# Attention: when the next batch's first stacks are loaded, after quad 2's maxima instead of after quad 0's key scores

## The chip, the cores and the metric

The kernel runs on one core of a Trainium2 chip. The metric is the time of one execution on the device in microseconds (us). The engines are TensorE (PE, with PEld for its weight loads), VectorE (DVE), ScalarE (ACT), GpSimd (POOL) and SyncE (SP), which here only issues DMAs.

## What is computed

A pre-normalized transformer block: attention with 16 heads over 16 batches of 512 rows of 256, then a feed-forward part with blockwise FP4 quantization.

```python
x_h = x.reshape(b, t, h, d).transpose(0, 2, 1, 3)
xw = jnp.einsum('bhtd,hde->bhte', x_h, w_att_val)
att = jnp.einsum('bhte,bhse->bhts', xw, x_h) / sqrt(d)
att = softmax(att, axis=-1)
vx = x @ wv_w.T + wv_b
o = jnp.einsum('bhts,bhsd->bhtd', att, vx)      # then o @ out_w.T + out_b
...
x = x + attention(layernorm(x))
x = x + ffn(layernorm(x))      # gate, up, silu, down; each operand quantized in blocks of 16
```

The change touches the attention part alone.

## The kernel before

A batch is one of the 16 inputs of 512 rows. Its 16 heads are worked in four **quads** of four heads (g = 0 to 3), and each quad in four **steps** (j = 0 to 3), one for each tile of 128 keys. The engines run unrolled programs of their own, side by side, and meet only at semaphores.

For each quad the scores are computed twice. First the *max scores* (L919, into one of four PSUM banks named `ring`): DVE takes the negated maximum of each row (L1189, `neg_max`). POOL splits these maxima into a high and a low part (L693), DVE turns them (L1198), and ACT stores them to memory (`store_maxima`, L1148, tensor `max_rows`) and loads them back in another shape (`load_maxima`, L1158, tile `max_stack`). Then the *key scores* (L927) with the maxima added by a second matmul (L930): ACT takes the exponential (L1071, `probs`) and PE weighs the values (L952).

The max scores run ahead: during quad g, from its step 1 on, PE computes those of quad g + 2 (`aimed`). So the max scores of quad 0 of the next batch begin at step 1 of quad 2 of this batch, ahead of that step's key scores. ACT stores the maxima of quad g + 1 at step 1 of quad g, and loads them at step 2 of quad g (after its copy of a bank at L1082); at step 2 of quad 1 it also issues the load of a later batch's x (`load_x`, L1162), for batches up to 12.

Both kinds of scores read two tiles of a quad, `x_stack[g]` and `q_stack[g]`: splits of x and of q, laid out by heads. They are made by POOL as `splits` (L727, L729), stored to memory by SP (`store_half`, L199), and loaded in the other layout by SP (`load_stacks`: two DMAs of 256 KB at L162 and four of 128 KB at L172, 1 MB in all). There is one buffer for each g, so the next batch's stacks can be loaded only when this batch's key scores of that quad are done, and PE waits for all six DMAs (`stack_loaded`, L911).

SP's queue in a batch is: for g = 0, the stores of x and q of the first half, the wait for the key scores of quad 0 (`s_ready`), the wait for those stores to land (in `load_stacks`, L177), quad 0's loads; for g = 1, the wait for quad 1's key scores, quad 1's loads, and the store of kept weights (L834); for g = 2, the stores of the second half and quad 2's loads; for g = 3, quad 3's loads and a load of weights (L829). All of SP's DMAs go through one hardware queue, ACT's through another.

Of the kernel before, what the change touches and what calls it, by code (L numbers as in the profile page):

```python
# [14 lines left out]
TT = T // P  # L15
# [3 lines left out]
QUAD = 4  # L19
QUADS = H // QUAD  # L20
PAIRS = 2
ROWS = 2
# [153 lines left out]
def load_stacks(sp, b, g, x_stack, q_stack, x_rows, q_rows, stored, stack_loaded):  # L176
    sp.wait_ge(stored[g * QUAD // HH], STORES * (b + 1))  # L177
    load_x_stack(sp, b, g, x_stack, x_rows, stack_loaded)
    load_q_stack(sp, b, g, q_stack, q_rows, stack_loaded)
# [255 lines left out]
def attention_block(nc, ctx, x, max_rows, w_gate, w_up, w_down, slabs, slabs_kept, first_x,  # L435
# [9 lines left out]
    def sem(name):  # L445
        return ctx.enter_context(nc.semaphore(name))
# [24 lines left out]
    max_loaded = [sem(f"max_loaded{g}") for g in range(QUADS)]  # L471
# [11 lines left out]
    s_ready, p_ready, pv_done, pv_begun, pv_ended, pv_summed = (  # L483
        sem(n) for n in ("s_ready", "p_ready", "pv_done", "pv_begun", "pv_ended", "pv_summed"))
# [54 lines left out]
    def stands(kind, b):  # L539


        if kind == LAST_ROWS:
            return isinstance(b, int) and b == B - 1
        if not isinstance(b, int):
            return True
        if b < 0 or b > B:
            return False
        return {0: kind not in FINISH and kind != "weights", B - 1: kind not in PREPARE and kind != "weights",
                B: False}.get(b, True)
# [67 lines left out]
    def quantizing(b):  # L617

        return not isinstance(b, int) or b < UNITS
# [36 lines left out]
    with nc.Block() as block:  # L656
# [146 lines left out]
        def _(sp):  # L803
# [5 lines left out]
            def store_half(c, a):  # L809
                store(c, a, x_rows, f"x{a}", (xh, xl, xl, xh))  # L810
                store(c, a, q_rows, f"q{a}", (qh, ql))

            def batch(b):
                last = isinstance(b, int) and b == B - 1
                for g in range(QUADS):
                    i = QUADS * b + g
                    if not last:
                        if g % 2 == 0:
                            store_half(b + 1, g // 2)
                        sp.wait_ge(s_ready, QUAD * TT * (i + 1))  # L820
                        load_stacks(sp, b + 1, g, x_stack, q_stack, x_rows, q_rows, stored, stack_loaded)
                        if g == 3 and quantizing(b + 1):
                            sp.wait_ge(w_quantized, b + 1)
                            load_weights(b + 1)
                        if g == 1 and stands("weights", b):
                            store_weights(b)

            def load_weights(b):
                sp.dma_start(w_raw[:, :].rearrange("p (s c) -> p s c", c=P),  # L829
                             slabs[bass.ds(UNIT * b, UNIT)].rearrange("s p c -> p s c")).then_inc(w_loaded, 16)  # L830

            def store_weights(b):
                sp.wait_ge(kept_used, use("weights", b, BY_ACT) + 1)
                sp.dma_start(slabs_kept[bass.ds(UNIT * (b - 1), UNIT)].rearrange("s p c -> p s c"),  # L834
                             w_turned[:, :].rearrange("p (s c) -> p s c", c=P)).then_inc(w_stored, 16)
# [38 lines left out]
            sp.wait_ge(w_copied, 16 * COPIES)  # L874
            load_weights(0)
            batch(0)
            with sp.Fori(1, B - 3) as b:
                batch(b)
            batch(B - 3)
            batch(B - 2)  # L880

# [925 lines left out]
```

## Time and profile before

| | |
|---|---|
| time, median of 3 runs | 1467.87 us (1466.48 to 1468.46) |
| profiled execution | 1475.75 us, its span 1473.8 us |
| busy, share of the span | PE 1425.4 us (97%), DVE 1264.4 (86%), ACT 865.5 (59%), POOL 659.0 (45%) |
| mean granted TensorE clock | 0.989 |
| DMA queues | SP's (q1) 137.22 MB, ACT's (q10) 10.37 MB; mean 100 GB/s |
| attention part | up to about 930 us; a batch takes some 56 us |

Times of rows are microseconds from the start of the span of the profiled execution. A wait is charged to what came last before the waiting instruction could start. The batches are counted from 0.

### The profile page before, as it was taken

Reading aid. Unit: us, or ns where it says so; the run is one execution under the profiler, and the core shown is the slowest. Engines: PE = TensorE matmul, PEld = TensorE weight load, DVE = VectorE, ACT = ScalarE, POOL = GpSimd, SP = SyncE. Lnnn points to the kernel's source line nnn. Section 1 sums busy time; section 2 is a strip of 40 time slices with the busy share of each in tenths; the row PEclk is TensorE's granted clock in tenths of the full one; section 3 lists DMA queues with packets and bytes.
Section 4 is the critical chain, followed back from the end, with each engine's and each line's share of the span. In section 5 each row is a group of like instructions: output and inputs, shape, how many; then the busy total and the mean of one; then the engine's idle time right before and its main releaser. Section 6 shows DMA issues by size and latency. Waiting matters only on the chain. (4 is left out here: it accounts for less than half of the span.)

```text
span 1473.8 us, 32381 instructions
## 1 busy us (share of the span) xinstructions
PE 1425.4 (97%) x8612; PEld 891.5 (60%) x8612; DVE 1264.4 (86%) x2652; ACT 865.5 (59%) x1731; POOL 659.0 (45%) x911
## 2 busy tenths in 40 slices
PE   6789999999999999999999999899999999999999
PEld 4445555555555555555555554577777777777776
DVE  6878888888888888888888887599999999999996
ACT  1667777777777767777777777533333333333332
POOL 2445545545545546546545523243434343433332
PEclk8999999999999999999999999999999999999999
DMA  7846456455455455465465353000000000000000
GB/s 204 234 132 190 123 144 180 122 154 180 122 154 168 132 155 161 123 166 162 125 165 145 117 145 84 0 15 15 18 14 18 14 18 14 18 14 18 14 18 22
DMA packets 99785, 148.09 MB, mean 100 GB/s; under 512 B 21024, under 2 KB 58272, under 8 KB 99744
## 3 DMA queue, kind: packets, MB, share of 16 engines
q1 hardware_dynamic: 82672, 137.22, 32.9%
q10 hardware_dynamic: 17072, 10.37, 3.0%
q8 instruction: 21, 0.34, 0.1%
q14 instruction: 20, 0.16, 0.0%
HBM read 85.02 MB, written 65.27 MB: 102 GB/s over the span
## 5 line engine op out<-in xcount | busy, mean ns | idle before, releaser
L1189 DVE TENSOR_REDUCE neg_max<-ring 128x1 f32<-128x512 f32 x1016 | 636.3, 680 | 96.2 <-PE ring L919 95.8
L1071 ACT ACTIVATE probs<-scores 128x512 f32<-128x512 f32 x1024 | 533.9, 604 | 184.3 <-PE scores L930 158.4
L1704 PE MATMUL gu_bank<-splits,f_x_T 128*128 128x352 f32 x1024 | 313.7, 459 | 0.1
L919 PE MATMUL ring<-x_stack,q_stack 64*128 64x512 f32 x1016 | 230.1, 449 | 24.5 <-DVE neg_max L1189 11.4
L952 PE MATMUL ring<-probs,v_quad 128*32 128x512 f32 x2048 | 247.9, 602 | 0.2
L1704 PEld LDWEIGHTS gu_bank<-splits,f_x_T 128*128 128x128 f32 x1024 | 189.6, 190 | 95.3 <-ACT f_x_T L1678 0.5
L927 PE MATMUL scores<-q_stack,x_stack 64*128 64x512 f32 x1024 | 207.9, 399 | 10.6 <-DMA max_stack<-max_rows 8.2
L919 PEld LDWEIGHTS ring<-x_stack,q_stack 64*128 64x128 f32 x1016 | 97.8, 186 | 177.2 <-DVE neg_max L1189 114.2
L930 PE MATMUL scores<-max_stack,max_ones 64*128 64x512 f32 x1024 | 203.9, 391 | 0.0
L1394 POOL TENSOR_TENSOR f_small<-f_small,eps 128x1 f32<-128x1 f32 x64 | 43.0, 671 | 296.0 <-DVE f_small L1361 296.0
L1663 ACT ACTIVATE h_T<-h_bank 128x256 f32<-128x256 f32 (+1 forms) x128 | 56.0, 487 | 169.9 <-PE h_bank L1718 169.9
L1726 PE MATMUL y_bank<-splits,h_T 128*128 128x256 f32 x640 | 148.9, 380 | 0.6 <-ACT h_T L1663 0.6
L952 PEld LDWEIGHTS ring<-probs,v_quad 128*32 128x32 f32 x2048 | 54.0, 109 | 124.5 <-issue 78.3
L1726 PEld LDWEIGHTS y_bank<-splits,h_T 128*128 128x128 f32 x640 | 116.7, 190 | 14.4 <-DVE x_all L1579 0.8
L927 PEld LDWEIGHTS scores<-q_stack,x_stack 64*128 64x128 f32 x1024 | 98.3, 186 | 32.7 <-ACT probs L1071 17.6
L693 POOL TENSOR_TENSOR max_cols<-neg_max,one 128x16 fp32r<-128x16 f32 x64 | 13.8, 216 | 227.0 <-DVE neg_max L1189 227.0
L930 PEld LDWEIGHTS scores<-max_stack,max_ones 64*128 64x128 f32 x1024 | 98.4, 186 | 18.9
L1445 POOL TENSOR_TENSOR hq<-h_level,h_scale 128x704 f32<-128x704 f32 x63 | 87.3, 1386 | 24.4 <-DVE h_level L1438 24.4
L716 POOL TENSOR_TENSOR pv_rows<-pv_more,pv_rows 128x512 f32<-128x512 f32 x63 | 80.8, 1282 | 36.0 <-ACT pv_more L1077 35.8
L1678 ACT ACTIVATE f_x_T<-x_bank 128x256 f32<-128x256 f32 x64 | 24.5, 383 | 117.8 <-PE x_bank L1692 117.8
L708 POOL TENSOR_TENSOR x_all<-x_all,out_bias 128x256 f32 (+1 forms) x64 | 47.1, 735 | 103.0 <-DVE x_all L1257 102.7
L1432 DVE SCALAR_TENSOR_TENSOR h_level<-h_mag,h_units 128x704 f32<-128x704 f32 x63 | 56.2, 891 | 39.7 <-ACT h_mag L1427 39.7
(144 smaller groups left out, 2014.1 us busy)
## 6 DMA issues: line engine op xcount, KB each, us to landing
x_rows<-splits SPq DMA_DIRECT2D x128, 256.0 KB, 3.9
x_stack<-x_rows SPq DMA_DIRECT2D x126, 256.0 KB, 4.0
q_stack<-q_rows SPq DMA_DIRECT2D x248, 128.0 KB, 4.0
q_rows<-splits SPq DMA_DIRECT2D x64, 256.0 KB, 2.2
out_dram<-x_all SPq DMA_DIRECT2D x64, 128.0 KB, 1.7
x_all<-in_L_attn_x_dram ACTq DMA_DIRECT2D x14, 512.0 KB, 6.9
w_raw<-slabs SPq DMA_DIRECT2D x14, 192.0 KB, 4.0
slabs_kept<-w_turned SPq DMA_DIRECT2D x14, 192.0 KB, 6.1
```

Source lines behind the costliest of these rows:

```text
L716: pool.tensor_tensor(pv_rows[g % 2][:, :], pv_more[:, :], pv_rows[g % 2][:, :], ALU.add)\
L919: pe.matmul(max_bank(b, g, ROWS * n + m)[:, :], row_tile(q_stack[q], m)[:, p, s * P:(s + 1) * P], row_tile(x_stack[q], m)[:, p, :], start= ...
L927: pe.matmul(scores[ROWS * p + m][:, :], row_tile(x_stack[g], m)[:, p, j * P:(j + 1) * P], row_tile(q_stack[g], m)[:, p, :], start=True, st ...
L930: pe.matmul(scores[ROWS * p + m][:, :], row_tile(max_ones, m)[:, 0, :], row_tile(max_stack[g % 2], m)[:, p, :], start=False, stop=True).th ...
L952: m = pe.matmul(bank(tile)[VW * h:VW * h + VW, :], v[q][:, j, h, :], probs[j][:, k, :], start=(j == steps[0]), stop=(j == steps[1]))
L1071: act.activation(probs[j][:, k, :], scores[k][:, :], ACT.Exp).then_inc(p_ready, 1)
L1189: dve.tensor_reduce(neg_max[q % 2][:, at:at + 1], max_bank(b, g, k)[:, :], AX.X, ALU.max, negate=True).then_inc(m_used, 1)
L1432: dve.scalar_tensor_tensor(out=level, in0=mag, scalar=SHIFT_MIN, in1=units, op0=ALU.max, op1=ALU.subtract)\
L1445: pool.tensor_tensor(blocks(out), blocks(level), spread(scale, BLK), ALU.mult).then_inc(done, 1)
L1663: act.activation(h_T[1 - u][:, first:end, :], h_bank[k][:, 0:end - first, :], ACT.Copy).then_inc(h_moved, 1)
L1704: m = pe.matmul(gu_bank[c][:, :], x_T[u][:, a, :], gate_up_T[:, a, c * CH:(c + 1) * CH], start=(a == 0), stop=(a == HALVES - 1))
L1726: m = pe.matmul(y_bank[:, :], h_T[u][:, k, :], down_T[k][:, :], start=(k == 0), stop=(k == len(SLICES) - 1))
```

## The change

SP's wait ahead of the loads of quad 0's stacks for batch b + 1 is another one: instead of "quad 0's key scores of batch b are done" it is "the maxima of quad 2 of batch b are back in `max_stack`" (`max_loaded[2]`). The other quads keep their wait. Nothing else is changed.

```diff
                     if not last:
                         if g % 2 == 0:
                             store_half(b + 1, g // 2)
-                        sp.wait_ge(s_ready, QUAD * TT * (i + 1))
+                        if g == 0:
+
+                            sp.wait_ge(max_loaded[2], 16 * ROWS * (b + 1))
+                        else:
+                            sp.wait_ge(s_ready, QUAD * TT * (i + 1))
                         load_stacks(sp, b + 1, g, x_stack, q_stack, x_rows, q_rows, stored, stack_loaded)
```

## Rows read from the trace of the kernel before

**Rows 1.** Waits of the whole run: us in total, times, longest us

```profile
PE ring L919 <- DMA q_stack<-q_rows: 9.1, 3, 4.3
PE scores L927 <- DMA max_stack<-max_rows: 8.2, 7, 1.8
PEld scores L927 <- DMA max_stack<-max_rows: 2.6, 2, 1.9
```

**Rows 2.** Timeline of PE, batch 5: start us, us, engine, line, op, times

```profile
345.44 1.92 PE L952 MATMUL ring<-probs,v_quad 128*32 128x512 f32 x16
...
351.16 0.40 PE L927 MATMUL scores<-q_stack,x_stack 64*128 64x512 f32 x2
...
354.30 0.50 PE L919 MATMUL ring<-x_stack,q_stack 64*128 64x512 f32 x2
```

**Rows 3.** Timeline of ACT, batch 5

```profile
344.02 0.55 ACTq L1148 DMA_DIRECT2D max_rows<-max_turned  x1
...
347.64 0.77 ACTq L1158 DMA_DIRECT2D max_stack<-max_rows  x2
348.69 0.42 ACTq L1162 DMA_DIRECT2D x_all<-in_L_attn_x_dram  x1
```

**Rows 4.** Timeline of ACT, batch 7

```profile
454.54 0.56 ACTq L1148 DMA_DIRECT2D max_rows<-max_turned  x1
...
459.49 0.65 ACTq L1158 DMA_DIRECT2D max_stack<-max_rows  x2
```

**Rows 5.** Timeline of PE, batch 7

```profile
455.96 1.92 PE L952 MATMUL ring<-probs,v_quad 128*32 128x512 f32 x16
...
463.20 0.50 PE L927 MATMUL scores<-q_stack,x_stack 64*128 64x512 f32 x2 [1.37 <-DMA max_stack<-max_rows]
...
466.41 0.50 PE L919 MATMUL ring<-x_stack,q_stack 64*128 64x512 f32 x2
```

**Rows 6.** Timeline of SP, batch 7: quad 0's x loads, then quad 1's

```profile
453.00 1.17 SPq L162 DMA_DIRECT2D x_stack<-x_rows  x2
...
459.44 1.14 SPq L162 DMA_DIRECT2D x_stack<-x_rows  x2
```

**Rows 7.** Tile q_stack, batch 7, quad 0: issues, landing

```profile
L172 SPq DMA_DIRECT2D q_stack<-q_rows x4: 370/415/535, 454.3 to 456.0; - x4
...
DMA to landing us min/median/max: 4.0/4.1/4.1
```

**Rows 8.** Tile q_stack, batch 7, quad 1

```profile
L172 SPq DMA_DIRECT2D q_stack<-q_rows x4: 316/370/443, 460.8 to 462.3; - x4
...
DMA to landing us min/median/max: 6.0/6.1/6.3
```

**Rows 9.** Tile q_stack, batch 13, quad 1

```profile
L172 SPq DMA_DIRECT2D q_stack<-q_rows x4: 421/458/583, 796.7 to 798.2; - x4
...
DMA to landing us min/median/max: 4.3/4.3/4.5
```

**Rows 10.** Timeline of SP, batch 0: quad 0's x loads, then quad 1's

```profile
65.03 1.15 SPq L162 DMA_DIRECT2D x_stack<-x_rows  x2
...
68.37 1.38 SPq L162 DMA_DIRECT2D x_stack<-x_rows  x2
```

**Rows 11.** Tile q_stack, batch 0, quad 0

```profile
L172 SPq DMA_DIRECT2D q_stack<-q_rows x4: 408/456/582, 66.2 to 67.8; - x4
...
DMA to landing us min/median/max: 6.1/6.3/8.2
```

**Rows 12.** DMA issues of the page: KB each, median us to landing

```profile
out_dram<-x_all SPq DMA_DIRECT2D x64, 128.0 KB, 1.7
```

**Rows 13.** Timeline of PE, batch 0

```profile
76.02 0.80 PE L919 MATMUL ring<-x_stack,q_stack 64*128 64x512 f32 x2 [4.02 <-DMA q_stack<-q_rows]
```

**Rows 14.** Timeline of PE, batch 13

```profile
800.99 3.61 PE L952 MATMUL ring<-probs,v_quad 128*32 128x512 f32 x16
```

**Rows 15.** Stretch: us, busy PE, PEld, DVE, ACT, POOL, granted clock, DMA share, GB/s

```profile
76.00:80.00 4.00, 3.98 (x14) 2.44 (x15) 2.31 (x5) 2.06 (x4) 0.23 (x1) 0.50 0.97 324
```

## The prediction

> **What bounds the kernel now.** I read the shares of busy time first: TensorE (PE) is busy 97% of the span, the VectorE (DVE) 86%. A share over the whole span doesn't say what one DMA wait is worth, so the next view is the waits of the whole run. The reader is to see there two DMA waits of PE: it waits for the maxima that come back from memory (8.2 us at the matmuls and 2.6 us at the weight loads, nine waits, 10.8 us in all), and three times for a stack of q (9.1 us) [rows 1].
>
> Then two batches side by side, each from the moment at which ACT issues the store of quad 2's maxima; I call that moment M. In batch 5 nothing waits: M is 344.02, the maxima's load is issued at 347.64 (M+3.6), the load of a later x at 348.69 (M+4.7), quad 2's key scores start at 351.16, and at 354.30 (M+10.3) PE runs the first max scores of quad 0 of the **next** batch, the first reader of the stacks that this change moves [rows 2, 3]. In batch 7 M is 454.54 and the maxima's load goes out only at 459.49, so the store took up to 4.9 us; the key scores start at 463.20 and the next batch's first max scores at 466.41, M+11.9 [rows 4, 5]. From the step at 455.96 that takes 10.45 us; the same steps of batch 5, from 345.44, take 8.86 us [rows 2, 5]. So a stall here of some 1.4 us costs about 1.6 us of the batch: nothing gives it back. That is my exchange rate, one for one, for every wait of PE below.
>
> What delays the store is plain in SP's queue: quad 0's loads for the next batch are issued at 453.00, the rest of quad 0's loads lands at 460.1, and quad 1's follow at 459.44 [rows 6, 7]. The change takes the first group out of the way of the maxima.
>
> **The change part by part.** (1) *Removed:* SP no longer waits for quad 0's last key scores. That wait is covered: the batch's second quad has to be running before quad 2's maxima can come back. Cost nothing.
>
> (2) *The maxima go undisturbed.* The 10.8 us of waits go, nearly all of them in these places. In batch 13 such a wait was followed by a group of value matmuls that took 3.61 us where the same group took 1.92 in batch 5; that 1.7 us goes too [rows 1, 2, 14]. Gain: 12.5 us at most, over 15 batches.
>
> (3) *The loads of quad 0 start later.* M+3.6 for the maxima's load as in batch 5, then its way. The traces bound that: below by the fastest landing on the page, 1.7 us [rows 12]; above by 3.7 us, from 459.49 to 463.20, when quad 1's loads ran beside it [rows 4, 5]. I take 2.2 us, near the fast end, because SP's queue is now empty meanwhile (SP itself stands in the new wait). With 0.1 us for SP to react, the loads go out at M+5.9, where batch 7 had them at M−1.5 [rows 4, 6].
>
> (4) *How long they take.* A quad's stacks are six DMAs, 1 MB, and PE waits for all of them. Four rows give the time from first issue to last landing; the q loads start 1.2 to 1.3 us behind the x loads [rows 6, 7]. Quad 0 in batch 7, alone: 453.00 to 456.0+4.1, 7.1 us [rows 6, 7]. Quad 1 in batch 13, where no x is loaded any more: 795.5 (796.7 less 1.2) to 798.2+4.5, 7.2 us [rows 9]. Quad 1 in batch 7, beside the load of x: 459.44 to 462.3+6.3, 9.2 us [rows 6, 8]. Quad 0 in batch 0, beside the load of x and with quad 1's loads right behind it at 68.37: 65.03 to 67.8+8.2, 11.0 us [rows 10, 11]. The new place has both neighbours: the load of x is issued at M+4.7, 1.2 us ahead of these loads, and quad 1's loads are queued right behind them, since their own condition is long true. So the nearest rows are the last two; I take 9.0 us, because part of x is moved before the stacks' bytes come, and keep 7.1 and 11.0 as ends. In batches 13 and 14 (no x) I take 7.8 us.
>
> The Trainium skill gives another price for the same megabyte ("DMA: Bandwidth & Descriptors", section "Anatomy of one DMA", a fit of 2.0 us plus bytes over 436 GB/s, stated for DMAs from GpSimd): an estimate by that page is 4.4 us, and the stacks would be there at M+10.3, just when PE asks. This case's trace speaks against it by 7.1 us for the least disturbed quad.
>
> (5) *The new wait.* Arrival at M+14.9, PE asks at M+10.3: 4.6 us in each of 12 batches (1 to 12), 55 us. Batches 13 and 14: M+13.7, 3.4 us each, 7 us. In batch 0 PE already waits for these stacks until 76.02, so only the later issue counts [rows 13]: 2 us. Batch 15 loads nothing. Sum 64 us. What is queued behind SP's waiting instruction is quad 1's loads, the store of the kept weights and the store of the second half of x; PE wants quad 1's stacks a whole quad later (some 14 us), and the second half's loads come after another store that is bound by GpSimd, so these have cover. PE is strictly in order here: behind its wait stand the key scores of the running quad, so ACT (exponentials) and DVE (maxima) run dry too.
>
> (6) *TensorE's clock.* During batch 0's wait the granted clock went down, and 76 to 80 us ran at 0.50, that is 1.2 GHz instead of 2.4: 4 us of work at half speed, 2.0 us lost [rows 15]. Batch 13's slow group is the same size (1.7 us). The new waits are as long as batch 0's. I take a fall in 11 of 14 batches at 1.8 us each: 20 us. Ends: none, and 14 times 2.1, 29 us.
>
> The Trainium skill describes this pattern ("TensorE: Matmul & The Clock Gate", section "HAM oscillation — how this bites in real kernels"): matmuls separated by DMA waits restart at the low clock each time. Batch 0's row agrees; batch 7's short wait shows no slow group after it.
>
> **Sum.** +64 −12.5 +20 = +71 us. The profiled run takes 1475.75 us (span 1473.8); that makes 1546.8. The profiled run is 7.9 us above the median of 1467.87, so against the median: 1539 us.
>
> **The rivals.**
> *A. Faster: the maxima's wait goes and nothing takes its place.* It decides at one point: the six loads must land within 4.4 us of M+5.9. Then only (2) is left, 1467.9 − 12.5, **1455 us**. For it: the waits for the maxima are real, and they are in this very place [rows 1, 5]; and the fit of the Trainium skill named above, "DMA: Bandwidth & Descriptors", would give just that. Against it: no row has less than 7.1 us. Chance 5%.
> *B. No effect.* The loads aren't what holds up the maxima, and the stacks are prefetched early enough. Then 1468 us. It would need the 10.3 us to be wrong; the loads would move by 7 us without a reader. Chance 4%.
> *C. A small loss.* The stacks land 7.1 us after issue, as quad 0's do now: a wait of 2.7 us, 14 times, 38 us, less 12.5, with the clock falling seldom (0 to 10 us): +25 to +36, **about 1498 us**. For it: the present row of exactly these loads. Chance 21%.
> *D. My forecast,* +45 to +95 us: chance 60%.
> *E. A heavy loss.* Batch 0's 11.0 us in every batch: 6.6 us, 14 times, 92 us, less 12.5, and the clock at 29: +109, **1577 us**. A second part may add to it: the traffic that is put off (quad 1's stacks, the half of x) meets the store of quad 3's maxima, at 1.2 us a meeting (8.2 us in seven waits) [rows 1]; I take none of it, since PE's own wait moves that store back as well. Chance 10%.
>
> **How the numbers follow.** The time is D's. To hold 8 in 10 the range takes D and most of C, and E's near part: 1498 to 1572 us. A measurement of this kernel can tell about 0.2% (3 us) from no change. Faster by more: A, 5%. Same: B, 4%. Slower: C, D and E, 91%.
>
> **What would show it.** In the profile after, in the waits of PE: the row for the maxima's stack (8.2 us) gone or near it; a row of the ring's max scores waiting for the stacks (x or q), 14 or 15 times, 3 to 6 us each, in place of three times. In SP's queue, quad 0's x loads about 5.9 us after the store of quad 2's maxima instead of 1.5 us before, with quad 1's some 3.5 us behind them. The granted clock of the attention part below its present level, with groups of value matmuls near 3.6 us. The q loads of quad 0 landing in 5.5 to 6.5 us instead of 4.1. The batches from 57 us to about 61. The feed-forward part unchanged.
> The forecast is wrong if the six loads land in under 6 us (A and C), if the wait for the maxima stays (then they were held up by something else), or if PE makes up for a wait of 4 us where it made up for none of 1.4.

## The result and the profile after

The changed kernel takes 1522.59 us (median of 4 runs, 1520.37 to 1524.88) against 1467.53 us (1466.48 to 1468.46) before: a ratio of 1.037, with a 95% interval of 1.035 to 1.039. It is slower by 55 us; the forecast was 71 us, 1539, with a range of 1498 to 1572. The profiled execution took 1524.11 us, its span is 1522.1. One execution of the first experiment below took 8051.6 us and is left out of its figures.

The shares of the page of after (busy us, share of the span, instructions):

```profile
span 1522.1 us, 32381 instructions
PE 1441.1 (95%) x8612; PEld 902.4 (59%) x8612; DVE 1266.0 (83%) x2652; ACT 867.2 (57%) x1731; POOL 659.4 (43%) x911
```

The work is the same to within 0.2% on DVE and ACT; PE is 16 us busier with as many instructions; the batch table below puts that down to the same work at a lower clock. What is new stands in the waits of the whole run (us in total, times, longest us):

```profile
PE ring L923 <- DMA q_stack<-q_rows: 50.8, 17, 4.6
PEld ring L923 <- DMA q_stack<-q_rows: 15.9, 5, 5.0
PE scores L931 <- DMA max_stack<-max_rows: 1.6, 2, 1.4
PEld scores L931 <- DMA max_stack<-max_rows: 0.5, 1, 0.5
```

Beside [rows 1]: the waits for the maxima have gone from 10.8 us to 2.1, and the matmul of the max scores now waits 17 times for the stacks, 50.8 us, where it waited three times, 9.1 us. (Lines are four further down than before.) One batch of after, number 5, in the order of the engines. ACT (start us, us): the store of quad 2's maxima at M = 360.05, their load, and the load of a later x:

```profile
360.05 0.55 ACTq L1152 DMA_DIRECT2D max_rows<-max_turned  x1
...
363.62 0.65 ACTq L1162 DMA_DIRECT2D max_stack<-max_rows  x2
364.54 0.42 ACTq L1166 DMA_DIRECT2D x_all<-in_L_attn_x_dram  x1
```

SP: quad 0's loads, and quad 1's right behind them:

```profile
365.82 1.17 SPq L162 DMA_DIRECT2D x_stack<-x_rows  x2
367.08 1.97 SPq L172 DMA_DIRECT2D q_stack<-q_rows  x4
369.38 1.14 SPq L162 DMA_DIRECT2D x_stack<-x_rows  x2
```

The tile q_stack of these loads, issues and landing:

```profile
L172 SPq DMA_DIRECT2D q_stack<-q_rows x4: 315/371/532, 367.1 to 368.7; - x4
DMA to landing us min/median/max: 4.4/4.5/4.9
```

PE: its wait, and the same step in batch 4, where the clock stayed up:

```profile
315.35 0.49 PE L923 MATMUL ring<-x_stack,q_stack 64*128 64x512 f32 x2 [3.15 <-DMA q_stack<-q_rows]
...
316.94 1.12 PE L971 MATMUL ring<-raw_x,qw_cols 128*128 128x512 f32 x2
317.90 0.60 PE L988 MATMUL ring<-ident,pv_rows 128*128 128x128 f32 x4
318.58 0.50 PE L923 MATMUL ring<-x_stack,q_stack 64*128 64x512 f32 x2
...
373.74 0.49 PE L923 MATMUL ring<-x_stack,q_stack 64*128 64x512 f32 x2 [3.34 <-DMA q_stack<-q_rows]
...
375.53 2.07 PE L971 MATMUL ring<-raw_x,qw_cols 128*128 128x512 f32 x2
377.40 1.06 PE L988 MATMUL ring<-ident,pv_rows 128*128 128x128 f32 x4
378.39 0.50 PE L923 MATMUL ring<-x_stack,q_stack 64*128 64x512 f32 x2
```

These lines show that the maxima are loaded at M+3.6, as in [rows 3]; the stacks are asked for at M+5.8 and are there at 368.7+4.9 = 373.6, M+13.55; PE begins 0.14 us later, at M+13.7, where the undisturbed batch of before began at M+10.3 [rows 2]. Then comes the second price: the same work, from the first pair of these max scores to the first pair of the next step, takes 3.23 us in batch 4 and 4.65 us in batch 5. The stretches of after (us, busy time of PE, PEld, DVE, ACT, POOL, granted clock, DMA share, GB/s) name the reason:

```profile
316.00:320.00 4.00, 3.92 (x28) 2.34 (x24) 3.97 (x10) 2.98 (x6) 2.30 (x3) 1.00 1.05 286
376.00:378.00 2.00, 2.00 (x5) 0.86 (x5) 1.20 (x4) 1.07 (x3) 0.84 (x1) 0.50 1.07 307
```

### The profile page after: what moved, and what is told of

Its sections match the earlier page's. It is cut to its first block and busy times, and to the rows that moved or that the text cites. A ratio compares the mean times of both kernels' runs of the same rounds, so it can differ in the third digit from the quotient of the medians.

```text
span 1522.1 us, 32381 instructions
## 1 busy us (share of the span) xinstructions
PE 1441.1 (95%) x8612; PEld 902.4 (59%) x8612; DVE 1266.0 (83%) x2652; ACT 867.2 (57%) x1731; POOL 659.4 (43%) x911
## 5 line engine op out<-in xcount | busy, mean ns | idle before, releaser
L923 PE MATMUL ring<-x_stack,q_stack 64*128 64x512 f32 x1016 | 234.9, 458 | 65.5 <-DMA q_stack<-q_rows 50.8
L934 PE MATMUL scores<-max_stack,max_ones 64*128 64x512 f32 x1024 | 207.7, 399 | 0.0
L1730 PEld LDWEIGHTS y_bank<-splits,h_T 128*128 128x128 f32 x640 | 116.7, 190 | 14.4 <-DVE x_all L1583 0.8
L1436 DVE SCALAR_TENSOR_TENSOR h_level<-h_mag,h_units 128x704 f32<-128x704 f32 x63 | 56.2, 892 | 39.5 <-ACT h_mag L1431 39.5
```

Of the source, the lines that this page charges most:

```text
L923: pe.matmul(max_bank(b, g, ROWS * n + m)[:, :], row_tile(q_stack[q], m)[:, p, s * P:(s + 1) * P], row_tile(x_stack[q], m)[:, p, :], start= ...
L934: pe.matmul(scores[ROWS * p + m][:, :], row_tile(max_ones, m)[:, 0, :], row_tile(max_stack[g % 2], m)[:, p, :], start=False, stop=True).th ...
L1436: dve.scalar_tensor_tensor(out=level, in0=mag, scalar=SHIFT_MIN, in1=units, op0=ALU.max, op1=ALU.subtract)\
L1730: m = pe.matmul(y_bank[:, :], h_T[u][:, k, :], down_T[k][:, :], start=(k == 0), stop=(k == len(SLICES) - 1))
```

## Where the 44 us of the batches come from

When every batch is read in this way, before and after, the times from one store of quad 2's maxima to the next one add up to 842.1 us before and 886.5 us after for batches 0 to 14, 44.4 us more. Three terms make them up. First, PE's first max scores of the next batch come later than the undisturbed M+10.3: in after by 39.5 us over batches 1 to 12 (2.8 to 3.5 each), 4.3 us in batches 13 and 14, 2.8 us in batch 0, in all 46.6 us. Second, before had such delays too: 9.8 us in batches 1 to 12, 4.1 in batch 0, 3.6 in batch 13 (its low clock within it), in all 17.5 us, and 2.0 us of low clock behind batch 0's wait. Third, the low clock of after: 11 of 15 batches have a stretch at 1.2 GHz about the end of the wait or behind it. From the next batch's first max scores to the next M, a batch with the clock up takes the same time before and after (44.7 us in batches 1 to 11); the batches with a low stretch take 1.1 to 1.5 us more, and 2.5 and 2.6 us in the two where it lasts twice as long, 17.3 us in all. 46.6 + 17.3 − 17.5 − 2.0 = 44.4 us, as measured.

The rest of the 48.3 us between the two spans is 4.0 us ahead of the first M (61.63 against 65.64), where the change has no effect: the low clock near the start lasted 30.7 us in this execution and 20.5 in the one of before, and 23.9 to 34.1 in the executions below, whatever the kernel.

## The experiments

M is always the issue of the store of quad 2's maxima. All times are against runs of the kernel before on the same chip; those had medians of 1467.1 to 1469.3 us. Times are medians of all executions; what is read by batch comes from the one profiled execution of each kernel, which can lie several us from its median.

**The same loads behind the store of the maxima instead of their load.** This parts the two ways in which quad 0's loads could hurt the maxima: on their way out and on their way back.

```diff
-                            sp.wait_ge(max_loaded[2], 16 * ROWS * (b + 1))
+                            sp.wait_ge(max_stored, 16 * (i + 3))
```

> Quad 0's loads wait for the store of quad 2's maxima to land instead of for their load (both engines' orders are otherwise those of the changed kernel). Theory (the stacks' arrival sets the loss; what is gained is that the store of the maxima runs alone): the store lands at M+2.0, the loads go out at M+2.2 and land in 7.0 us, at M+9.2 to 9.6, ahead of the moment at which PE asks (M+10.3); no wait for the stacks after batch 0, no low clock after it, batches of 55.0 us, so about 10 us below the kernel before: 1457 us. Rival 1 (the load of the maxima suffers beside the stacks' loads as much as the store did): key scores of quad 2 at M+8.5 instead of M+7.1, 1.4 us in each of 15 batches, about 1478 us. Rival 2 (the store alone doesn't matter): as the kernel before, 1467 us.

Measured: 1480.7 us, 1.0087 of before (1.0059 to 1.0114). The theory fell, since it had the loads of the stacks leave the maxima alone and land in 7.0 us. The result is near the 1478 us of rival 1, but only half of it is rival 1's: the key scores of quad 2 come at M+7.8 (mean of batches 1 to 12), not at M+8.5. The other part, which neither named, is that the stacks come late as well. Batch 6, ACT, then SP, then the tile q_stack, then PE:

```profile
404.11 0.56 ACTq L1152 DMA_DIRECT2D max_rows<-max_turned  x1
...
407.69 0.67 ACTq L1162 DMA_DIRECT2D max_stack<-max_rows  x2
408.62 0.47 ACTq L1166 DMA_DIRECT2D x_all<-in_L_attn_x_dram  x1
```

```profile
406.23 1.18 SPq L162 DMA_DIRECT2D x_stack<-x_rows  x2
```

```profile
L172 SPq DMA_DIRECT2D q_stack<-q_rows x4: 315/371/527, 407.5 to 409.1; - x4
DMA to landing us min/median/max: 4.0/4.7/6.9
```

```profile
412.30 0.49 PE L931 MATMUL scores<-q_stack,x_stack 64*128 64x512 f32 x2 [0.89 <-DMA max_stack<-max_rows]
...
416.16 0.50 PE L923 MATMUL ring<-x_stack,q_stack 64*128 64x512 f32 x2 [0.59 <-DMA q_stack<-q_rows]
```

The maxima's load, issued at 407.69, is used at 412.30, 4.6 us later, because the stacks' bytes are now under way beside it: the way back suffers as the way out did. And the stacks, issued at 406.23, are there only at 409.1+6.9 = 416.0: 9.8 us. The load of x, issued 2.4 us **behind** them, costs them nearly 3 us here: in batches 13 and 14, which load no x, they took 7.1 and 6.8 us, and those batches 54.8 and 55.0 us. Over batches 1 to 12 the stacks took 9.3 us (mean), and 7.3 us in the run further down that has x moved as well. The loss is paid in two waits per batch, mostly under 1 us each.

**An earlier condition: quad 1's key scores.**

```diff
-                            sp.wait_ge(max_loaded[2], 16 * ROWS * (b + 1))
+                            sp.wait_ge(s_ready, QUAD * TT * (i + 2))
```

> Quad 0's loads wait for the key scores of quad 1 to be done (M+4.8), 0.9 us ahead of the changed kernel's condition (M+5.7). Theory (one for one with the arrival of the stacks): issue at M+5.0, arrival at M+12.7, so each of 14 batches gains 0.8 us against the changed kernel: 1511 us, with as many falls of the clock (11) or a few less. Rival (the loads now meet the load of the maxima, which lands at M+5.5): the key scores of quad 2 wait, the gain is gone: 1522 us or more.

Measured: 1504.0 us, 1.025 of before (1.022 to 1.029). Issue at M+4.9, arrival at M+12.4 to 13.2 in batches 1 to 12, the maxima undisturbed (key scores at M+7.1 in all batches), so the rival is out. The gain over the changed kernel is 18 us instead of 11: the arrival gives some 7 us, and the low clock came with four of these waits (13.7 us of low clock in all) instead of eleven (44.4). In these two executions a wait that is shorter by half a microsecond has cost the clock far less often.

**PE kept at work during the wait,** by 22 matmuls whose results are overwritten.

```diff
                 elif at == 0:
+                    if q == 0:
+                        for semaphore, count in room(tiles, b):
+                            pe.wait_ge(semaphore, count)
+                        for _ in range(11):
+                            for m in range(ROWS):
+                                pe.matmul(max_bank(b, g, ROWS * n + m)[:, :], row_tile(q_stack[2], m)[:, 0, 0:P],
+                                          row_tile(x_stack[2], m)[:, 0, :], start=True, stop=True)
                     pe.wait_ge(stack_loaded[q], STACK * (c + 1))
```

> The changed kernel, with 22 matmuls more (11 pairs, about 2.6 us of PE's time) into the two banks that the next max scores overwrite, ahead of PE's wait for the next batch's quad 0 stacks; no result is changed. Theory (the low clock after the wait costs 1.4 us, or 2.7 where it lasts twice as long, 11 times): the falls after these waits go, the max scores of the next batch start at the same M+13.5, batches with a fall (59.5 us) come down to those without (58.2): about 16 us less, 1506 us. Rival (the clock costs nothing, since other waits end last): unchanged, 1522 us. Rival (the fill delays PE): 2.6 us in each of 15 batches more, 1560 us.

Measured: 1505.3 us, 1.025 of before (1.022 to 1.028): 17.3 us less than the changed kernel. PE, batch 5:

```profile
365.37 2.79 PE L921 MATMUL ring<-x_stack,q_stack 64*128 64x512 f32 x22
368.72 0.50 PE L930 MATMUL ring<-x_stack,q_stack 64*128 64x512 f32 x2 [0.55 <-DMA q_stack<-q_rows]
```

The real max scores still begin at M+13.5 (mean of batches 1 to 12), batches 1 to 14 take 57.2 to 58.9 us, and the granted clock is at full speed from 55 us to the end. So the low clock was worth 17 us, as the batch table said, and the matmuls without use gave all of it back.

**The load of a later x moved away from quad 0's stacks.**

```diff
-                    if (g, j) == (1, 2) and prepared(b + 3):
+                    if (g, j) == (2, 3) and prepared(b + 3):
```

> The changed kernel, with the load of a later batch's x issued by ACT at the end of step 3 of quad 2 instead of step 2 of quad 1, so that it isn't beside quad 0's stacks. Theory (that load makes the stacks land in 7.7 us instead of 7.1): arrival 0.6 us earlier in 12 batches, 7 us less: 1515 us. Rival (quad 1's loads behind them are what adds, or nothing does): unchanged, 1522 us. The forecast's own figure for it (1.9 us from 7.1 to 9.0) would give 22 us less, 1500 us.

Measured: 1509.9 us, 1.029 of before (1.026 to 1.031), 12.7 us less than the changed kernel. The tile q_stack in batch 5 (first x load at 362.70):

```profile
L172 SPq DMA_DIRECT2D q_stack<-q_rows x4: 315/371/532, 364.0 to 365.6; - x4
DMA to landing us min/median/max: 4.0/4.1/4.3
```

365.6+4.3−362.70 = 7.2 us; over batches 2 to 12 it is 6.9 to 7.2 where the changed kernel has 7.3 to 8.0 (batch 1 took 8.8 here, a single one, not explained). Summed over the batches, that is the 7 us expected. The rest is the clock again, low with six waits instead of eleven in the profiled execution: some 5 us between the medians, some 10 between the two profiled executions, which lie 16.7 us apart. Quad 1's loads still run right behind, so they cost nothing here.

**A second dose of the delay: quad 2's first key scores as the condition.**

```diff
-                            sp.wait_ge(max_loaded[2], 16 * ROWS * (b + 1))
+                            sp.wait_ge(s_ready, QUAD * TT * (i + 2) + QUAD)
```

> Quad 0's loads wait for the key scores of quad 2's step 0 (done at about M+8.1), 2.5 us behind the changed kernel's condition: a second dose of the same delay. Theory (one for one, and a longer wait lets the clock fall more surely): issue M+8.3, arrival M+16.0, 2.5 us more in each of 15 batches, 37 us, and the clock down after nearly all waits, 5 us: 1566 us. Rival (PE, ACT and DVE make up for a long wait out of the slack between them): less than 1545 us.

Measured: 1562.5 us, 1.064 of before (1.062 to 1.067). This is PE in batch 4, with the clock low from the first matmul on (0.79 us for a pair that takes 0.5):

```profile
325.21 0.79 PE L923 MATMUL ring<-x_stack,q_stack 64*128 64x512 f32 x2 [5.23 <-DMA q_stack<-q_rows]
```

Issue at M+8.4, arrival at M+15.2 to 15.9, the clock low with all 15 waits, in eleven of them for twice the time. Nothing makes up for a longer wait. The stacks took 7.1 us here (mean), as they do with x moved; the load of x was issued 3.9 us ahead of them.

**Both edits at once: behind the store, and x moved.** (Diffs as above.)

> Quad 0's loads wait for the store of quad 2's maxima (M+2.1), and the load of a later x is moved to step 3 of quad 2. In the run with the store gate alone the batches without a load of x (13 and 14) had their stacks at M+9.1 and 8.8, key scores at M+7.25 and 54.9 us a batch, those with it 11 to 12, up to M+8.3, and 56.0 to 56.9 us. Theory (the loads of x and of the stacks together are too much for this stretch): all batches come to 55.0 us, 12 x 1.5 us less than the 1481 us of the store gate alone: 1463 us, 4 to 5 us below the kernel before. Rival (the batches 13 and 14 are quick for another reason): 1478 us or more. Rival (the load of x disturbs as much in its new place, beside the traffic of the second half): about 1470 us.

Measured: 1471.8 us, 1.0032 of before (1.0019 to 1.0045). The stacks land at M+9.1 to 10.4 and PE waits for them in no batch; the 8.9 us against the store gate alone are that. But the maxima are still used at M+7.3 to 8.9 (in batches 0 to 14), with 14 waits at the matmuls in the whole run:

```profile
PE scores L931 <- DMA max_stack<-max_rows: 8.3, 14, 1.6
```

The batches 1 to 12 take 55.8 us (mean) where 55.0 was expected: the way back beside the stacks is the part that moving x does not remove. Batches 13 and 14 of the store gate alone, from which the 55.0 was taken, were no safe model for it: here batch 14 uses its maxima at M+8.0.

**The kernel before with x moved.**

> The kernel before with the load of a later x moved to step 3 of quad 2, nothing else. Theory (in the kernel before it is quad 0's loads that hold up the store of quad 2's maxima, and quad 1's loads their return): the maxima's load is still issued at M+4 to M+5, PE still waits for it in about nine batches: 1466 us, within 0.2% of the kernel before. Rival (the load of x is what makes these maxima late): the waits go and it comes to 1458 us.

Measured: 1464.1 us, 0.9966 of before (0.9949 to 0.9982): a little faster than both kernels, and between the theory, which said 1466, and the rival with 1458. The store of the maxima is as late as ever (4.2 us to its landing, mean of batches 1 to 12; 4.5 before, 1.96 in the changed kernel), yet in the profiled execution the waits are nearly gone:

```profile
PE scores L927 <- DMA max_stack<-max_rows: 2.8, 3, 1.3
PEld scores L927 <- DMA max_stack<-max_rows: 0.8, 2, 0.6
```

In 13 of its batches 1 to 14 the key scores come at M+7.1 to 7.2, the batches take 54.5 to 55.0 us, and only batch 11, whose maxima were loaded latest, waits. That execution was the quickest of the twelve (1458.81 us, 5.3 below their median), and the profiled one of before was 7.9 above its own, so the two traces show more than the 5 us between the medians; how many batches wait in a typical execution is not shown. ACT, then SP, in batch 11:

```profile
666.48 0.55 ACTq L1148 DMA_DIRECT2D max_rows<-max_turned  x1
671.52 0.65 ACTq L1158 DMA_DIRECT2D max_stack<-max_rows  x2
```

```profile
671.39 1.14 SPq L162 DMA_DIRECT2D x_stack<-x_rows  x2
```

Here the maxima's load is issued 0.13 us behind quad 1's loads. This order is what tells the batches apart: in the traces of before, of this run and of the next, each load of quad 2's maxima (batches 1 to 14) issued ahead of quad 1's loads (up to M+4.7) lands within 1.8 to 2.4 us, and each one issued at about their time or behind them (M+4.9 on) takes 3.1 to 4.0 us and makes PE wait. The two store-gate runs move the order by an edit: there quad 0's loads are issued 0.9 to 1.5 us ahead of the maxima's load, and it takes 3.6 to 5.2 us in batches 0 to 14.

**The kernel before with x one step later,** at the end of step 3 of quad 1.

```diff
-                    if (g, j) == (1, 2) and prepared(b + 3):
+                    if (g, j) == (1, 3) and prepared(b + 3):
```

> The kernel before with the load of a later x issued one step later (end of step 3 of quad 1) instead of four steps later as in the run that came to 1464 us. Theory 1 (in the kernel before, ACT's instructions for this load, between the maxima's load and the exponentials of quad 1's step 3, are what is saved): 1464 us as there, key scores of quad 2 at M+7.1 in nearly all batches. Theory 2 (the bytes of x beside quad 1's stacks are what delays the maxima): the bytes still come there, though 3 us later, after the maxima have landed at M+6; also 1464 us, but quad 1's stacks take over 8 us where they took 7.0. If neither is true (the store of the maxima differs by chance between the runs): 1468 us.

Measured: 1464.0 us, 0.998 of before (0.9965 to 0.9996). Four of its batches 1 to 12 wait for the maxima, which were loaded at M+4.9 or later; the other eight have their max scores at M+10.3, also where the maxima's load was issued only at M+4.4 to 4.6, while the kernel before needs 10.6 to 11.1 for a load at M+4.2 to 4.7 that PE did not wait for. So ACT's issue of the load of x, ahead of the exponentials, costs 0.3 to 0.8 us in such a batch (theory 1). Quad 1's stacks take 9.0 to 10.9 us in batches 1 to 12, as theory 2 said; nobody waits for them. Why the store is under 4.9 us in one batch and over it in the next stays open: its neighbours are the same in each.

**The changed kernel with the fill and with x moved.**

> The changed kernel with both edits: the 22 matmuls more ahead of PE's wait for the stacks, and the load of a later x moved to step 3 of quad 2. Theory (the loss of the changed kernel is the arrival, at one for one, plus the clock, and nothing else): no low clock in the batches, the next batch's max scores at M+12.8 instead of M+13.6, batches of 57.5 us, 9 us less than the 1505 us of the fill alone: 1496 us. Rival (the two remedies overlap, each taking the other's gain): 1505 us.

Measured: 1498.9 us, 1.022 of before (1.019 to 1.025), 23.7 us less than the changed kernel and 6 less than the fill alone. The max scores begin at M+12.9, batches 1 to 14 take 57.2 to 57.7 us, and there is no stretch of low clock. The fill covers 17 us, x 6: they add up, and x's further 5 us by itself were the clock, which the fill already has. What remains, 2.6 us in each batch, is the late start of the loads. The fill is now as long as the wait: in batch 12 the stacks are there at M+12.6, and PE, which begins at M+12.9, had first to end it. That is part of why the run stays above the 1496 us of its theory.

## Why the prediction was right, step by step

(1) SP's old wait cost nothing when it went, as said: the batch table leaves nothing for it.

(2) *The maxima undisturbed.* Right in place and size. The store lands in 1.96 us instead of 4.5, key scores at M+7.1 to 7.2 in batches 0 to 14; the waits fell by 8.7 us, and by the batch table the delays of batches 1 to 14 (13.4 us, low clock included) are gone, against the 12.5 forecast. What the step did not see is that part of it is ACT's issue of the load of x: 0.3 to 0.8 us in the batches without a DMA wait. All this is read from a profiled execution of before that was 7.9 us above the median, so in a typical one it may be less.

(3) *The later start.* Forecast M+5.9, measured M+5.35 to 5.85. The maxima's load took about 2.0 us against 2.2.

(4) *How long the loads take.* This is the term that was mis-sized: 9.0 us forecast, 7.3 to 8.0 measured in batches 1 to 12 (mean 7.7), and 7.2 and 7.0 against 7.8 in 13 and 14. The step took the rows with the load of x issued 0.7 to 1 us behind the stacks as the nearest ones [rows 8, 11]. It saw that in the new place that load is 1.2 us ahead of them, but for that it took off only 0.2 us from the shorter of the two, 9.2 us. The runs show how much the order of the issues counts: with the load of x 1.2 us ahead the stacks took 7.7 us (mean), with it 0.4 us ahead, in the run with quad 1's key scores as the condition, 8.0; in before, quad 1's stacks took 9.0 to 10.5 with it at their side or up to 1.1 us behind them, and in the run with the store gate they took 8.4 to 10.0 with it 2.4 us behind. Moving it away gave 0.7 us a batch. Quad 1's loads right behind, the other half of its reason, cost nothing (6.9 to 7.2 us with x moved). The fit that the Trainium skill gives for one DMA ("DMA: Bandwidth & Descriptors", section "Anatomy of one DMA") makes 4.4 us of this megabyte as an estimate; in this form no batch agrees, and the shortest took 7.0 us. With six DMAs issued by SP, 2.7 to 2.9 us pass between the first issue and the last alone.

(5) *The new wait.* For batches 1 to 14 forecast 62 us, measured 43.8: 39.5 for 55 (the 1.3 us of step 4, twelve times), 4.3 for 7. In batch 0 the forecast had the sign wrong: it said 2 us more, and the change gained 3.3. The loads went out 2.1 us later, counted from M, but took 7.5 us for 11.0, so the max scores began at M+13.1 instead of M+14.4, and the low clock behind that wait (2.0 us) was gone. The exchange of one for one held, within 0.1 us a batch before and after; only in the run with the store gate did four batches (5, 8, 9 and 10) take 0.3 to 0.7 us more than it gives. Batch 4 of after waits 3.2 us longer than the undisturbed batch and takes 58.2 us for 54.96.

(6) *The clock.* Forecast 11 falls at 1.8 us, 20 us; measured 11 falls (of 15 batches), 17.3 us from the batch table, 17.3 us by the fill. That the count came out at 11 exactly is luck; the other three executions of after had mean clocks of 0.976 to 0.979 where the profiled one had 0.975. The Trainium skill's description ("TensorE: Matmul & The Clock Gate", section "HAM oscillation — how this bites in real kernels") has the low clock come back with each such wait; the trace agrees in 11 of the 15 batches, and in four the clock stayed up.

*The sum.* In the same parts: 43.8 (new waits) − 3.3 (batch 0) − 13.4 (the maxima) + 17.3 (clock) = 44.4 us for the +71 of the forecast. Of the 27 us between them some 17 are step 4's term, 5 are batch 0, 3 the clock. The two profiled executions differ by 48.4 us (1524.11 − 1475.75), these 44.4 and the 4.0 of the start. The medians differ by 55, because the profiled run of before lay 7.9 us above its median and that of after only 1.5 above; the forecast took the 7.9 for both, which hid 6 us of its error. That its 71 us look near to the measured 55 is in this part luck.

Rival A (faster) needed the loads within 4.4 us and fell at that point. B fell with it. C (about 1498) was near with the length of the loads, 7.1 against 7.7, and a clock that falls seldom, which was wrong; D holds with 55 us of its 45 to 95. E's 11.0 us was batch 0's alone, and in after batch 0 itself took 7.5. Its second part did not come: the store of quad 3's maxima landed in 2.66 us (mean of batches 1 to 12) for 2.60 before.

## What to carry to other kernels

A prefetch that is put off to protect another transfer has a reader of its own: before moving it, read from the trace how long after its issue that reader asks, and how long the transfer takes with the neighbours of its new place, in the order in which they will be issued. Where the reader is the engine that sets the pace, add the clock: a wait of 3 us on TensorE cost 3 us and, most times, 1.4 more. A small transfer on the critical path was quick here when it was issued ahead of the large ones. What gained in the end, 3 to 5 us of 1467, was none of the new conditions, but to move the issue of an unrelated load off the engine that must go on, and away from the small transfer.

## What the runs showed of the hardware that was not expected

- A small load (16 KB in two DMAs) issued just ahead of 1 MB of loads landed in 1.8 to 2.4 us; just behind them in 3.1 to 4.0 us (before and the two runs of it with x moved). A store of 16 KB took 1.96 us in after and 3.6 to 5.1 us in before, behind 1 MB of loads issued 1.5 us ahead of it.
- The 512 KB load on ACT's queue cost the 1 MB on SP's queue 0.7 us when it was issued 1.2 us ahead. Issued at their side or up to 1.1 us behind, it cost quad 1's stacks of before some 2 to 3.5 us (9.0 to 10.5 against 6.6 to 7.0 with x moved), and 2.4 us behind, some 2 us (9.3 against 7.3, means of the two store-gate runs).
- How often the clock fell rose with the wait, in one profiled execution of each kernel (delays of PE past M+10.3, means of batches 1 to 12): with 4 of 15 waits at 2.8 us, 6 of 15 at 2.7 us, 11 of 15 at 3.3 us, 15 of 15 at 5.4 us. In after it also fell with the two shortest delays (2.1 and 2.3 us, batches 14 and 13), so a shorter wait is no sure remedy.
